# AdaLN transformer layer on one core: another order of the work in the first of eight attention turns

## The chip, the cores and the metric

The kernel runs on one core of a Trainium2 chip. The metric is the device time of one launch in microseconds (us). Three runs of the kernel before took 980.37 to 980.84 us, with a median of 980.65.

Engines: PE is TensorE (matrix products and transposes), DVE is VectorE, ACT is ScalarE, POOL is GpSimd, and SP issues most of the DMAs. Each engine works through its own list of instructions in written order; semaphores join them.

## The reference, cut to what matters

```python
# x: (2, 1024, 256) f32; 16 query heads in 4 groups, 4 key/value heads, D = 128
mod = (silu(c) @ wmod).reshape(2, 6, 1, -1)             # c: (2, 256)
sa, ca, ga, sb, cb, gb = (mod[:, i] for i in range(6))
ga = (2 * (ga >= 0) - 1) * maximum(abs(ga), 0.25)        # gb in the same way
h = layernorm(x) * (1 + ca) + sa
qkv = einsum('bsh,ph->bsp', h, weight_qkv)               # per group: 4 q, k, v
scores = einsum('bsgqd,btgd->bgqst', q, k) / sqrt(128)   # causal
attn = softmax(scores)
x = x + ga * (einsum('bgqst,btgd->bsgqd', attn, v) @ weight_proj.T)
h = layernorm(x) * (1 + cb) + sb
h = fwht(h * SU_ug) / 64
h = silu(h @ W_gate.T * s_gate) * (h @ W_up.T * s_up)
h = fwht(h * SU_dp) / 64
x = x + gb * (h @ W_down.T * s_down)
```

## The kernel before, in words

Every f32 factor of a product is split in a high part (fp32r) and a low part (the rest), and a product is three matmuls: high by high, high by low, low by high (`three`, L922 to L924). Names end in `_hi` and `_lo`.

The attention goes in eight turns, one for each batch and key/value head. A turn has twelve chunks (`C`): a chunk is 512 positions of one q head, of k or of v, made by six matmuls of 512 columns from h_hi, h_lo, w_hi and w_lo. ScalarE takes the high part from PSUM (L588 to L592) and VectorE the low part (L786, L788). Then come, for each tile of 128 queries and each of 4 heads, the scores (`S`: PE L1031 to L1037, DVE adds the mask and finds the maximum in L820, ACT makes the exp in L603, POOL divides by the sum in L493 and L496), the transposes of the probabilities (`T`: PE L1046, ACT L623, DVE L824), the products with v (`V`) and the projection (`Y`). The score tiles alternate between two PSUM areas of two banks each, so a score waits for the exp of the second one before it. v is transposed by `VT` (PE L999, ACT L581, DVE L794).

What order these take is a list of steps, `WALK`, built by `walk()` (L64 to L137). All four compute engines go through the same list, and each does its own part of a step. What stands before the loop over `WALK` in an engine's code is done first.

Turn 0 has extra work ahead. SP loads x in four quarters, the modulation weights in two parts and the first qkv weights w_raw. PE makes the first modulations (SA, CA), and the first batch's LayerNorm runs in two halves of 512 positions, each half in two slots: DVE takes statistics (`ln_front`, L714 to L722) and normalises (`ln_normalise`, L730), POOL makes rstd (L430), PE transposes (L946), ACT modulates (`ln_modulate`, L568), DVE makes h_hi (`ln_high`, L738) and POOL h_lo (`ln_low`, L437). POOL makes w_hi (`split_w`, L441) and DVE w_lo (L750). Chunk 0 needs w_lo and the first half's h_lo. The second half's transposes are the step `L0`. Three more steps belong to turn 0: `M` makes the other modulations on PE (L933, L970) and DVE copies them (L765, L766); `G` are the gates (DVE, L773 to L777, with `guard`, L704 to L707), which ga_row and so the scaling of the projection weights need; `WM` is that scaling (POOL, `scale_wp`, L476) and `WP` the split of the scaled weights (POOL, `split_wp`, L484 and L486). `gates` also waits for the five small loads, the mask among them.

After the eight turns the feed-forward part follows, which the change doesn't touch.

## Time and profile before

| | |
|---|---|
| median of three runs | 980.65 us |
| the profiled execution | 982.66 us |
| its span in the trace | 980.9 us |
| mean granted TensorE clock | 0.993 of full |
| PE busy | 941.8 us, 96% |
| DVE busy | 645.0 us, 66% |
| ACT busy | 514.3 us, 52% |
| POOL busy | 462.9 us, 47% |

The span is the time from the first to the last instruction that the profiler saw; the device time is a little longer. A row of a timeline gives start, duration, engine, line, operation, output and inputs, their shapes, and in brackets how long the engine sat idle before it and what it waited for. `PEclk` is the clock that TensorE was granted, as a share of 2.4 GHz. "ps" is a PSUM bank, and "prob" is a large buffer that in turn 0 also holds the modulation weights and the second LayerNorm slot.

### The profile page before, as it was taken

To read this page: it belongs to the slowest core of one execution; us is meant where nothing else is said; L and a number is where in the kernel's file an instruction comes from. 1 tells how busy PE (TensorE), PEld (TensorE's weight loads), DVE (VectorE), ACT (ScalarE), POOL (GpSimd) and SP (SyncE) were. 2 spreads that over 40 slices of the span, in tenths; PEclk is the share of its full clock that TensorE was granted. 3 is DMA by queue.
4 is the path that set the end of the run, shared out by engine and by line. 5 is a ranking of instruction groups with operands and counts; after the bars stand their busy time and mean duration, and the time that the engine had idled before them with its cause. 6 is when DMAs were issued, how large, how long until landed. Compare 5 with 4: busy or idle time off the path is not lost.

```text
span 980.9 us, 14522 instructions
## 1 busy us (share of the span) xinstructions
PE 941.8 (96%) x5344; PEld 818.8 (83%) x5344; DVE 645.0 (66%) x1298; ACT 514.3 (52%) x1069; POOL 462.9 (47%) x601
## 2 busy tenths in 40 slices
PE   2969999999999999999999999999999999999997
PEld 2859888888888888888888888888888887888885
DVE  5367756775677567757774787477747776864553
ACT  1346645665566456646664666366646665331221
POOL 2165634673477357725672567266716674120000
PEclk9998999999999999999999999999999999999999
DMA  8000000000000000000000000000000002000000
GB/s 303 1 1 22 1 33 1 22 2 33 1 22 1 33 1 22 1 33 1 22 4 29 2 22 21 12 1 23 1 1 1 1 20 78 1 3 20 21 21 21
DMA packets 9522, 21.14 MB, mean 22 GB/s; under 512 B 1264, under 2 KB 5488, under 8 KB 9328
## 3 DMA queue, kind: packets, MB, share of 16 engines
q1 hardware_dynamic: 8592, 19.66, 5.9%
q8 instruction: 40, 0.66, 0.3%
q10 hardware_dynamic: 864, 0.60, 0.2%
q14 instruction: 26, 0.21, 0.1%
HBM read 18.17 MB, written 2.10 MB: 21 GB/s over the span
## 4 chain that ended last, share of the span: by engine, by line
PE 87%; DVE 7%; ACT 3%; DMA 1%; issue 1%; POOL 0%; SPq 0%; DVEq 0%; ACTq 0%
PE ps L922 18%; PE ps L924 18%; PE ps L923 18%; PE ps L1046 11%; PE ps L1031 6%; PE ps L1037 6%; PE ps L1034 6%; DVE ps L820 3%; ACT prob L603 2%; DVE pt_lo L824 1%; DMA x<-in_x 1%; PE ps L946 1%; PE ps L999 1%; PE ps L1091 1%; ACT pt_hi L623 0%
## 5 line engine op out<-in xcount | busy, mean ns | idle before, releaser
L493 POOL TENSOR_TENSOR rinv<-rsum,mone 128x1 f32<-128x1 f32 x256 | 143.4, 560 | 290.6 <-ACT prob L603 290.4
L623 ACT ACTIVATE pt_hi<-ps 128x512 fp32r<-128x512 f32 x288 | 171.8, 597 | 136.2 <-PE ps L1046 135.1
L824 DVE TENSOR_TENSOR pt_lo<-ps,pt_hi 128x512 fp32r<-128x512 f32 x288 | 198.3, 689 | 64.4 <-ACT pt_hi L623 62.7
L603 ACT ACTIVATE prob<-ps,nmax 128x1024 f32<-128x1024 f32 (+7 forms) x256 | 189.8, 742 | 83.8 <-DVE nmax L820 83.0
L820 DVE CUSTOM_DVE_ANT_0 ps<-ps,mask_f 128x1024 f32<-128x1024 f32 (+7 forms) x256 | 193.9, 763 | 51.7 <-PE ps L1037 49.8
L496 POOL TENSOR_SCALAR prob<-prob,rinv 128x1024 f32<-128x1024 f32 (+7 forms) x256 | 192.5, 752 | 53.9 <-POOL rinv L493 53.9
L1046 PE MATMUL ps<-ident,prob 128*128 128x128 f32 x1152 | 172.2, 273 | 5.4 <-DVE pt_lo L824 5.4
L1046 PEld LDWEIGHTS ps<-ident,prob 128*128 128x128 f32 x1152 | 141.7, 141 | 24.8 <-DVE pt_lo L824 5.6
L922 PE MATMUL ps<-pt_hi,v_hi 128*128 128x512 f32 x288 | 134.6, 467 | 0.0
L924 PE MATMUL ps<-pt_hi,v_lo 128*128 128x512 f32 x320 | 126.5, 395 | 0.0
L1031 PE MATMUL ps<-k_hi,q_hi 128*128 128x512 f32 (+4 forms) x384 | 114.0, 351 | 6.8 <-ACT prob L603 6.8
L923 PE MATMUL ps<-pt_lo,v_hi 128*128 128x512 f32 x288 | 113.7, 395 | 0.0
L1037 PE MATMUL ps<-k_hi,q_lo 128*128 128x512 f32 (+4 forms) x384 | 111.3, 344 | 0.0
L1034 PE MATMUL ps<-k_lo,q_hi 128*128 128x512 f32 (+4 forms) x384 | 110.9, 343 | 0.0
L922 PE MATMUL ps<-h_hi,w_hi 128*128 128x512 f32 x192 | 79.1, 412 | 11.2 <-POOL h_lo L437 11.2
L1031 PEld LDWEIGHTS ps<-k_hi,q_hi 128*128 128x128 f32 x384 | 70.1, 190 | 23.4 <-ACT prob L603 10.6
L788 DVE SCALAR_TENSOR_TENSOR q_lo<-ps,q_hi 128x512 fp32r<-128x512 f32 x64 | 44.2, 691 | 62.0 <-ACT q_hi L592 62.0
L1034 PEld LDWEIGHTS ps<-k_lo,q_hi 128*128 128x128 f32 x384 | 71.3, 190 | 7.8
L592 ACT ACTIVATE q_hi<-ps 128x512 fp32r<-128x512 f32 x64 | 38.3, 599 | 74.9 <-PE ps L924 74.9
L924 PE MATMUL ps<-h_hi,w_lo 128*128 128x512 f32 x192 | 76.0, 396 | 0.0
L923 PE MATMUL ps<-h_lo,w_hi 128*128 128x512 f32 x192 | 75.9, 395 | 0.0
L1037 PEld LDWEIGHTS ps<-k_hi,q_lo 128*128 128x128 f32 x384 | 71.0, 189 | 5.3
(133 smaller groups left out, 1618.3 us busy)
## 6 DMA issues: line engine op xcount, KB each, us to landing
w_raw<-in_wqkv SPq DMA_DIRECT2D x8, 768.0 KB, 4.2
wp_raw<-in_wproj SPq DMA_DIRECT2D x8, 512.0 KB, 3.5
x<-in_x SPq DMA_DIRECT2D x4, 512.0 KB, 10.9
prob<-in_wug SPq DMA_DIRECT2D x4, 512.0 KB, 4.8
out_y<-prob SPq DMA_DIRECT2D x4, 512.0 KB, 2.9
prob<-in_wmod SPq DMA_DIRECT2D x1, 1024.0 KB, 11.6
raw_down<-in_wdn SPq DMA_DIRECT2D x1, 1024.0 KB, 12.6
prob<-in_wmod SPq DMA_DIRECT2D x1, 512.0 KB, 5.5
```

Of the source, the lines that this page charges most:

```text
L496: g_.tensor_scalar(row(i, h), row(i, h), rinv[:, at, h:h + 1], 1.0, ALU.mult, ALU.mult).then_inc(prob_done, 1)
L603: a_.activation(row(i, h).rearrange("p (a n) -> p a n", a=nb), score_banks(i, h).rearrange("p (a n) -> p a n", a=nb)[:, :, 0:w], ACT.Exp, ...
L623: a_.activation(pt_hi[:, n % 3, :], ring(t, "T", n), ACT.Copy).then_inc(pth_done, 1)
L820: v_.tensor_tensor_reduce(scores, scores, late, -1.0, 3.0e38, ALU.add, ALU.min, nmax[:, place(n), h:h + 1]).then_inc(max_done, 1)
L824: v_.tensor_tensor(pt_lo[:, n % 3, :], ring(t, "T", n), pt_hi[:, n % 3, :].bitcast(F32), ALU.subtract).then_inc(ptl_done, 1)
L922: mm(dst, w_h, r_h, start=start, stop=False)
L923: mm(dst, w_h, r_l, start=False, stop=False)
L924: return mm(dst, w_l, r_h, start=False, stop=stop)
L1031: mm(dst[:, a * CH:a * CH + wide], q_hi[:, h, q_at], k_hi[:, a * w:a * w + wide], start=True, stop=False)
L1034: mm(dst[:, a * CH:a * CH + wide], q_hi[:, h, q_at], k_lo[:, a * w:a * w + wide], start=False, stop=False)
L1037: last = mm(dst[:, a * CH:a * CH + wide], q_lo[:, h, q_at], k_hi[:, a * w:a * w + wide], start=False, stop=True)
L1046: last = tr(ring(t, "T", n)[:, q * P:(q + 1) * P], row(i, q, j * P, (j + 1) * P), ident[:, :])
```

## The change

Only turn 0 takes another order.

- Both v chunks go to the end of the turn's chunks, and chunks 0 to 7 use the four score banks, chunks 8 to 11 the two banks of `X`. Before, chunks went round six banks.
- The second half's LayerNorm: DVE takes its statistics only after it has made the first half's h_hi and h_lo; its transposes stand behind chunk 1, its h_hi and h_lo in a new step `LH0` behind chunk 2.
- The first batch's h_lo is made by DVE, no longer by POOL.
- DVE copies the first modulations before it makes w_lo, and POOL makes w_hi before the second half's rstd.
- `M` stands behind chunk 3 (before: behind chunk 7), `G` behind chunk 6, and `WM` and `WP` behind chunk 7 (before, these three stood behind the first score of tile 6).
- Each of the last four chunks is followed by a score of tile 7; the four small scores of tile 0 all stand behind `VT`.
- SP's queue: the mask, which ACT's queue had, stands behind the modulation weights; quarters 2 and 3 of x and raw_down stand behind the first projection weights.
- The wait for x's last quarters moves from the gates to step `LF`, that for the small loads on ACT behind the attention.

```diff
@@ -43,7 +43,7 @@
 QS = [[("q", h, half) for h in range(QPG)] for half in range(2)]
-CHUNKS_FIRST = [("k", 0, 0)] + QS[0] + [("v", 0, 0), ("k", 0, 1)] + QS[1] + [("v", 0, 1)]
+CHUNKS_FIRST = [("k", 0, 0)] + QS[0] + [("k", 0, 1)] + QS[1] + [("v", 0, 0), ("v", 0, 1)]
 CHUNKS_LATER = [("k", 0, 0), ("k", 0, 1)] + QS[1] + [("v", 0, 0), ("v", 0, 1)] + QS[0]
@@ -75,14 +75,15 @@
     s7 = scores(0, NT - 1)
-    out = [(0, "C", 0, 0), (0, "L0", 0, 0)] + [(0, "C", c, 0) for c in range(1, 8)] + [(0, "M", 0, 0)]
-    out += [(0, "C", c, 0) for c in (8, 9)] + [s7[0], (0, "C", 10, 0), s7[1], (0, "C", 11, 0), s7[2], s7[3]]
-    out += scores(0, 0)[:2]
+    out = [(0, "C", 0, 0), (0, "C", 1, 0), (0, "L0", 0, 0), (0, "C", 2, 0), (0, "LH0", 0, 0), (0, "C", 3, 0), (0, "M", 0, 0)]
+    out += [(0, "C", c, 0) for c in (4, 5, 6)] + [(0, "G", 0, 0), (0, "C", 7, 0), (0, "WM", 0, 0), (0, "WP", 0, 0)]
+    for h in range(QPG):
+        out += [(0, "C", 8 + h, 0), s7[h]]
     for t in range(TURNS):
...
         rest = [(t - 1, "Y", i, 0) for i in WINDOWS[-1][::-1]] if t else []
-        out += rest[:1] + [(t, "VT", 0, 0)] + s0[2 + (t > 0):] + [s6[0]] + rest[1:]
-        out += [(t, "WP", 0, 0)] if t else [(t, "G", 0, 0), (t, "WM", 0, 0), (t, "WP", 0, 0)]
+        out += rest[:1] + [(t, "VT", 0, 0)] + s0[3 if t else 0:] + [s6[0]] + rest[1:]
+        out += [(t, "WP", 0, 0)] if t else []
         behind, due = [], []
@@ -297,8 +298,8 @@
         def bank(t, c):
-            if t == 0:
-                return X[c % 6 - 4] if c % 6 >= 4 else S[c % 6 // 2][:, c % 2 * CH:(c % 2 + 1) * CH]
+            if t == 0 and c >= 8:
+                return X[c % 2]
             return S[c % 4 // 2][:, c % 2 * CH:(c % 2 + 1) * CH]
@@ -388,14 +389,16 @@
             load_wmod(1)
-            load_x(2)
-            load_x(3)
-            sp.dma_start(raw_down[:, :], wdn).then_inc(raw_s[4], 16)
+            sp.dma_start(mask_f[:, :], mask_in).then_inc(small_s, 16)
             for t in range(TURNS):
...
                              wproj[t % NKV, :, :].rearrange("p (h n) -> p h n", h=QPG)).then_inc(wpraw_s, 16)
+                if t == 0:
+                    load_x(2)
+                    load_x(3)
+                    sp.dma_start(raw_down[:, :], wdn).then_inc(raw_s[4], 16)
                 if t + 1 < TURNS:
@@ -441,18 +444,15 @@
             for r, slots in enumerate(LN_SLOTS):
-                pool.sem_inc(ln[r]["lo"], slots)
+                if r:
+                    pool.sem_inc(ln[r]["lo"], slots)
             pool.wait_ge(pool_self, 1)
...
                 ln_rstd(0, 0, 0, slot)
+            pool.wait_ge(wraw_s, 16)
+            split_w()
             for slot in range(2):
...
-
-            pool.wait_ge(wraw_s, 16)
-            split_w()
-            for g in range(NP // 2):
-                for slot in range(2):
-                    ln_low(0, 0, g, slot)
@@ -552,7 +552,6 @@
             a_.activation(sc[:, 1, :, :], sc[:, 0, :, :], ACT.Exp, scale=-1.0).then_inc(silu_e, 1)
-            act.dma_start(mask_f[:, :], mask_in).then_inc(small_s, 16)
             act.dma_start(su_u[:, :], su_ug).then_inc(small_s, 16)
@@ -571,10 +570,8 @@
             act.wait_ge(mod_ok, 1)
-            for g in range(NP // 2):
-                for slot in range(2):
-                    ln_modulate(0, 0, g, slot)
-            act.wait_ge(small_s, 5 * 16)
+            for slot in range(2):
+                ln_modulate(0, 0, 0, slot)
             def v_high(t):
@@ -609,6 +606,9 @@
                     exps()
+                if what == "L0":
+                    for slot in range(2):
+                        ln_modulate(0, 0, 1, slot)
                 if what == "VT":
@@ -627,6 +627,7 @@
+            act.wait_ge(small_s, 5 * 16)
             a_.activation(sc[:, 1, :, :], sc[:, 0, :, :], ACT.Silu)
@@ -682,6 +683,7 @@
                 dve.sem_inc(s, n)
+            dve.sem_inc(ln[0]["lo"], LN_SLOTS[0])
             dve.sem_inc(g32_s, 2)
@@ -737,27 +739,32 @@
+            def ln_low(r, b, g, slot):
+
+                n, block, _, _ = ln_step(r, b, g, slot)
+                dve.wait_ge(ln[r]["hi"], n + LN_SLOTS[r] + 1)
+                at = slice(block * P, (block + LP) * P)
+                v_.tensor_tensor(h_lo[:, :, at], h32[slot][:, :, :], h_hi[:, :, at].bitcast(F32), ALU.subtract).then_inc(ln[r]["lo"], 1)
+
...
+
+            dve.wait_ge(mod_mm, 1)
+            link(v_.tensor_copy(cols[:, 0:2, :, :], S[0][:, 0:2 * KH * B].rearrange("p (v k b) -> p v k b", v=2, k=KH)))
+            v_.tensor_scalar(cols[:, CA, :, :], cols[:, CA, :, :], 1.0, None, ALU.add).then_inc(mod_ok, 1)
+            dve.wait_ge(w_hi_s, 1)
+            v_.tensor_tensor(w_lo[:, :, :], w_raw[:, :, :], w_hi[:, :, :].bitcast(F32), ALU.subtract).then_inc(w_ready, 1)
+            for slot in range(2):
+                ln_high(0, 0, 0, slot)
+                ln_low(0, 0, 0, slot)
             dve.wait_ge(x_in_s[1], 16)
...
-
-            dve.wait_ge(w_hi_s, 1)
-            v_.tensor_tensor(w_lo[:, :, :], w_raw[:, :, :], w_hi[:, :, :].bitcast(F32), ALU.subtract).then_inc(w_ready, 1)
-
-            dve.wait_ge(mod_mm, 1)
-            link(v_.tensor_copy(cols[:, 0:2, :, :], S[0][:, 0:2 * KH * B].rearrange("p (v k b) -> p v k b", v=2, k=KH)))
-            v_.tensor_scalar(cols[:, CA, :, :], cols[:, CA, :, :], 1.0, None, ALU.add).then_inc(mod_ok, 1)
-            for slot in range(2):
-                ln_high(0, 0, 0, slot)
             for slot in range(2):
                 ln_normalise(0, 0, 1, slot)
-            for slot in range(2):
-                ln_high(0, 0, 1, slot)
@@ -776,7 +783,6 @@
                                       ws_d[:, :].unsqueeze(2).to_broadcast([P, KH, B]), ALU.mult))
-                dve.wait_ge(x_in_s[2], (B - 1) * NC_B * 16)
@@ -800,11 +806,16 @@
                     modulations()
+                if what == "LH0":
+                    for slot in range(2):
+                        ln_high(0, 0, 1, slot)
+                        ln_low(0, 0, 1, slot)
                 if what == "G":
...
                 if what == "LF":
+                    dve.wait_ge(x_in_s[2], (B - 1) * NC_B * 16)
                     dve.wait_ge(add_done, this(add_done, t, 0))
@@ -960,8 +971,6 @@
-                for c in (4, 5):
-                    pe.wait_ge(*evicted(0, c))
                 pe.wait_ge(wmod_s[1], 16)
@@ -978,12 +987,12 @@
                     pe.wait_ge(ln[1]["lo"], t + 1)
-                if t == 0 and c % 6 == 0:
-                    pe.wait_ge(ln[0]["lo"], LN_SLOTS[0] + 2 + c // 3)
-                if t == 0 and c == 10:
+                if t == 0 and c in (0, 5):
+                    pe.wait_ge(ln[0]["lo"], LN_SLOTS[0] + (4 if c else 2))
+                if t == 0 and c in (8, 9):
                     pe.wait_ge(mods_read, 1)
-                if c >= (4 if t else 6):
-                    pe.wait_ge(*evicted(t, c - (4 if t else 6)))
+                elif c >= 4:
+                    pe.wait_ge(*evicted(t, c - (2 if t == 0 and c > 9 else 4)))
                 at = {"q": h, "k": QPG, "v": QPG + 1}[what] * D
@@ -1019,8 +1028,7 @@
                     elif e <= QPG and not t:
-                        for c in (2 * e + 4, 2 * e + 5) if e <= 2 else (e + 6,):
-                            pe.wait_ge(*evicted(t, c))
+                        pe.wait_ge(*evicted(t, e + 5))
                     if e > 2:
```

The next rows are lists of instructions with their waits, in an engine's order.

DVE before chunk 0, kernel before: from the second half's statistics to its normalising; h32 and prob are the two slots' modulated values.

```order
L722 TENSOR_SCALAR vare<-mv 128x2 [waits ln0_aggr]
L750 TENSOR_TENSOR w_lo<-w_raw,w_hi 128x1536 [waits w_hi_done]
L753 COPY cols<-ps0 128x8 [waits mod_multiplied]
L754 TENSOR_SCALAR cols<-cols 128x4 [waits dve_self]
L738 CAST h_hi<-h32 128x2x256 [waits ln0_h32]
L738 CAST h_hi<-prob 128x2x256 [waits ln0_h32]
L730 TENSOR_SCALAR xhat<-x,mv,rstd 128x256 [waits ln0_rstd,ln0_tr]
```

The same place in the changed kernel.

```order
L732 TENSOR_SCALAR prob<-x,mv,rstd 128x256
L756 COPY cols<-ps0 128x8 [waits mod_multiplied]
L757 TENSOR_SCALAR cols<-cols 128x4 [waits dve_self]
L759 TENSOR_TENSOR w_lo<-w_raw,w_hi 128x1536 [waits w_hi_done]
L740 CAST h_hi<-h32 128x2x256 [waits ln0_h32]
L747 TENSOR_TENSOR h_lo<-h32,h_hi 128x2x256 [waits ln0_hi]
L740 CAST h_hi<-prob 128x2x256 [waits ln0_h32]
L747 TENSOR_TENSOR h_lo<-prob,h_hi 128x2x256 [waits ln0_hi]
L716 BN_STATS stats<-x 128x6 [waits x_loaded1]
```

The columns now stand ahead of w_lo, h_lo is new on DVE, and the second half's statistics begin behind it.

POOL from the first rstd on, kernel before.

```order
L430 TENSOR_TENSOR rstd<-vare,mhalf 128x2 [waits ln0_vare] x3
L441 TENSOR_SCALAR w_hi<-w_raw 128x1536 [waits w_raw_loaded]
L437 TENSOR_TENSOR h_lo<-h32,h_hi 128x2x256 [waits ln0_hi]
L437 TENSOR_TENSOR h_lo<-prob,h_hi 128x2x256 [waits ln0_hi]
L437 TENSOR_TENSOR h_lo<-h32,h_hi 128x2x256 [waits ln0_hi]
L437 TENSOR_TENSOR h_lo<-prob,h_hi 128x2x256 [waits ln0_hi]
L493 TENSOR_TENSOR rinv<-rsum,mone 128x1 [waits exp_done]
```

The changed kernel, the same place.

```order
L433 TENSOR_TENSOR rstd<-vare,mhalf 128x2 [waits ln0_vare]
L444 TENSOR_SCALAR w_hi<-w_raw 128x1536 [waits w_raw_loaded]
L433 TENSOR_TENSOR rstd<-vare,mhalf 128x2 [waits ln0_vare] x2
L476 TENSOR_TENSOR wp_raw<-wp_raw,ga_row 128x1024 [waits wp_raw_loaded,gate_ready]
L484 TENSOR_SCALAR wp_hi<-wp_raw 128x1024 [waits y_done,wp_scaled]
L486 TENSOR_TENSOR wp_lo<-wp_raw,wp_hi 128x1024 [waits wp_hi_done]
L493 TENSOR_TENSOR rinv<-rsum,mone 128x1 [waits exp_done]
```

w_hi stands ahead of the second two rstd, the four h_lo are gone, and the scaling and the split of the projection weights stand ahead of the first score's normalising.

DVE at the gates, kernel before: behind the maximum of tile 6's first score (896 columns).

```order
L820 ISA ps0,nmax<-ps0,mask_f 128x2x448 [waits scores_done]
L820 ISA nmax 128x1
L773 TENSOR_SCALAR cols<-cols 128x4 [waits small_loaded,modulations_read]
L704 SCALAR_TENSOR_TENSOR sum_down<-ga_row 128x512
L705 TENSOR_SCALAR sum_down<-sum_down 128x512 [waits dve_self]
L706 TENSOR_SCALAR sum_down<-ga_row 128x512 [waits dve_self]
L707 SCALAR_TENSOR_TENSOR ga_row<-sum_down 128x512 [waits dve_self]
```

DVE at the gates in the changed kernel: from q_lo of chunk 6 to that of chunk 7.

```order
L794 SCALAR_TENSOR_TENSOR q_lo<-ps1,q_hi 128x512 [waits qkv_hi]
L780 TENSOR_SCALAR cols<-cols 128x4 [waits small_loaded,modulations_read]
L706 SCALAR_TENSOR_TENSOR sum_down<-ga_row 128x512
L707 TENSOR_SCALAR sum_down<-sum_down 128x512 [waits dve_self]
L708 TENSOR_SCALAR sum_down<-ga_row 128x512 [waits dve_self]
L709 SCALAR_TENSOR_TENSOR ga_row<-sum_down 128x512 [waits dve_self]
L706 SCALAR_TENSOR_TENSOR sc<-cols 128x4
L707 TENSOR_SCALAR sc<-sc 128x4 [waits dve_self]
L708 TENSOR_SCALAR sc<-cols 128x4 [waits dve_self]
L709 SCALAR_TENSOR_TENSOR cols<-sc 128x4 [waits dve_self]
L784 TENSOR_TENSOR cols<-cols,ws_d 128x4 [waits dve_self]
L794 SCALAR_TENSOR_TENSOR q_lo<-ps1,q_hi 128x512 [waits qkv_hi,dve_self]
```

The gates now stand between two chunks' low parts, and the wide maxima stand behind them.

## Rows read from the trace of the kernel before

**Rows 1.** The page's busy times: us, share of the span, instructions.
```profile
PE 941.8 (96%) x5344; PEld 818.8 (83%) x5344; DVE 645.0 (66%) x1298; ACT 514.3 (52%) x1069; POOL 462.9 (47%) x601
```

**Rows 2.** PE's timeline, 7 to 79 us: start, us, engine, line, what.
```profile
7.31 3.54 PE L933 MATMUL ps<-sc,prob 128*128 128x2 f32 x16 [7.31 <-DMA prob<-in_wmod]
...
11.60 1.06 PE L946 MATMUL ps<-ident,prob 128*128 128x128 f32 x4
23.82 0.76 PE L922 MATMUL ps<-h_hi,w_hi 128*128 128x512 f32 x1 [11.16 <-POOL h_lo L437]
...
37.62 2.73 PE L933 MATMUL ps<-sc,prob 128*128 128x2 f32 x24
...
42.16 0.99 PE L922 MATMUL ps<-h_hi,w_hi 128*128 128x512 f32 x1
...
46.40 0.62 PE L1031 MATMUL ps<-k_hi,q_hi 128*128 128x512 f32 x2
...
47.76 0.39 PE L922 MATMUL ps<-h_hi,w_hi 128*128 128x512 f32 x1
...
73.84 1.11 PE L1046 MATMUL ps<-ident,prob 128*128 128x128 f32 x4 [5.40 <-DVE pt_lo L824]
...
78.98 0.50 PE L922 MATMUL ps<-pt_hi,v_hi 128*128 128x512 f32 x1
```

**Rows 3.** DVE's timeline before chunk 0.
```profile
12.19 0.75 DVE L714 BATCH_NORM_STATS2 stats<-x 128x6 f32<-128x256 f32 x2 [2.23 <-DMA x<-in_x]
...
17.04 1.76 DVE L750 TENSOR_TENSOR w_lo<-w_raw,w_hi 128x1536 fp32r<-128x1536 f32 x1 [2.25 <-POOL w_hi L441]
...
20.17 0.43 DVE L738 CAST h_hi<-h 128x512 fp32r<-128x512 f32 x1 [1.09 <-ACT h L568]
```

**Rows 4.** POOL's timeline: w_hi, then scaling and split of projection weights.
```profile
15.54 1.48 POOL L441 TENSOR_SCALAR w_hi<-w_raw 128x1536 fp32r<-128x1536 f32 x1
...
68.47 2.34 POOL L476 TENSOR_TENSOR wp_raw<-wp_raw,ga_row 128x1024 f32<-128x1024 f32 x1
71.00 1.05 POOL L484 TENSOR_SCALAR wp_hi<-wp_raw 128x1024 fp32r<-128x1024 f32 x1 [0.19 <-issue]
72.13 2.35 POOL L486 TENSOR_TENSOR wp_lo<-wp_raw,wp_hi 128x1024 fp32r<-128x1024 f32 x1
```

**Rows 5.** SP's timeline: the issue of w_raw.
```profile
2.27 0.47 SPq L388 DMA_DIRECT2D w_raw<-in_wqkv  x1
```

**Rows 6.** DMAs: queue, count, KB each, us from issue to landing.
```profile
w_raw<-in_wqkv SPq DMA_DIRECT2D x1, 768.0 KB, 7.9
...
mask_f<-in_mask ACTq DMA_DIRECT2D x1, 512.0 KB, 7.9
```

**Rows 7.** DVE's timeline: the first wide maximum, and the gates.
```profile
47.96 1.23 DVE L820 CUSTOM_DVE_ANT_0 ps<-ps,mask_f 128x1024 f32<-128x1024 f32 x1
...
65.20 0.17 DVE L773 TENSOR_SCALAR cols<-cols 128x4 f32<-128x4 f32 x1
...
67.52 0.16 DVE L704 SCALAR_TENSOR_TENSOR sc<-cols 128x4 f32<-128x4 f32 x1
...
68.57 2.27 DVE L706 TENSOR_SCALAR sc<-cols 128x4 f32<-128x4 f32 x1
...
71.07 0.99 DVE L777 TENSOR_TENSOR cols<-cols,ws_d 128x4 f32<-128x4 f32 x1
```

**Rows 8.** ACT's timeline: the mask's issue, the first wide exp.
```profile
2.48 0.33 ACTq L555 DMA_DIRECT2D mask_f<-in_mask  x1
...
49.81 1.11 ACT L603 ACTIVATE prob<-ps,nmax 128x1024 f32<-128x1024 f32 x1
```

**Rows 9.** Windows: stretch, length, busy time by engine, PEclk, DMA share, GB/s.
```profile
58.50:62.00 3.50, 3.27 (x17) 2.98 (x15) 1.89 (x7) 1.65 (x4) 2.88 (x6) 0.51 0.00 0
68.50:72.00 3.50, 0.00 (x0) 0.00 (x0) 3.40 (x4) 0.00 (x0) 3.31 (x3) 1.00 0.00 0
74.00:78.50 4.50, 4.50 (x15) 3.83 (x16) 2.24 (x4) 2.45 (x6) 3.56 (x5) 0.50 0.41 117
```

## The prediction

> **What bounds the kernel now.** I read the busy shares first: TensorE (PE) is busy for 941.8 of 980.9 us [rows 1], so 39 us are not matmul time, and a change of order alone can win only among them and among stretches at half clock. Then PE's timeline of the first 80 us, because the change touches only turn 0 (every other turn keeps its chunk order, banks and waits). There PE makes the modulations at 7.31, the eight LayerNorm transposes until 12.66, and then does nothing for 11.16 us, until chunk 0 at 23.82 [rows 2]. In the first 79 us it also stops for 5.40 us before the transposes at 73.84 [rows 2], and it has short stops in the scores' chain. The engines' own timelines say why. In the first gap everything hangs on VectorE (DVE), in its written order: statistics of the second half's x (its data land at 12.19), the low half of the weights at 17.04, the columns of the modulations, then h_hi at 20.17 [rows 3]. GpSimd (POOL) made w_hi only at 15.54, since the second half's rstd stands ahead of it [rows 4]; but w_raw was issued at 2.27 and landed 7.9 later, at 10.17 [rows 5, 6]. The second gap is DVE in the gates from 65.20 to 72.06 [rows 7], while scores, their maxima and pt_lo queue behind.
>
> I count up to one landmark: the start of the second P·V group of turn 0, at 78.98 [rows 2]. Behind it PE runs full in both versions, so what the landmark gains, the end gains.
>
> **First part: until chunk 0.** The mask's 0.5 MB were moving from 2.48 to 10.38 [rows 6, 8], beside x, the first modulation weights and w_raw. Now the mask goes behind them. Total bytes until 10.4 fall by about a sixth, so w_raw lands between 9.0 and 10.17 instead of at 10.17; the first modulations may start up to 0.6 earlier. DVE has normalised the first half ahead of PE's transposes and is free. PE's modulations end at 10.85 (7.31+3.54), its transposes at 12.66 [rows 2]. Now: columns copied and 1 added by about 11.3; w_hi (1.48 [rows 4]) from 9.2 to 10.7 at best, to 11.9 at worst; w_lo (1.76 [rows 3]) then ends at 13.1, at worst 13.8. ScalarE's modulation of slot 0, which follows its transposes, lies beside w_lo. Then DVE: h_hi 0.43 [rows 3] and h_lo, twice. DVE's h_lo has no row; by w_lo's 1.76 for 1536 columns it is 0.59 to 0.7 for 512 (estimate from rows 3). Twice 0.43+0.69 with three short waits on itself is 2.5. Chunk 0 starts at 15.6 (15.0 to 16.4) instead of 23.82: **8.2 us earlier**.
>
> **Second part: the chunks.** A chunk is six matmuls of 512 columns. PE starts one score of six such matmuls at 46.40 and the next chunk at 47.76 [rows 2], so 1.36 for six at full clock; at half clock twice, 2.6. Chunk 0 starts cold, as before: I take 4.3 us at half clock, nearly the 4.5 us behind the other long stop [rows 9], then full. Chunks 0 and 1 take 4.85; eight transposes at full clock 1.0 (four take 1.06 cold [rows 2], so eight 2.1, halved); chunks 2 and 3 2.7; the later modulations 4.5, as before (37.62 to 42.16 [rows 2]); and the two chunks behind them 4.24, since the two before (42.16 to 46.40 [rows 2]) ran at half clock behind the same small matmuls; chunks 6 and 7 2.7. That is 20.1, so chunk 7 ends at 35.7. The same place was 43.8 with the clock's dip moved to where it now is: the 8.2 stay.
>
> What hides the moved work: DVE ends h_lo at 15.5. The second half's fronts take 2.6 (from 12.19 [rows 3] to 14.8, one rstd of 0.7 ahead of w_hi's 15.54 [rows 4]), to 18.1; rstd and normalising end at 19.6; PE reaches these transposes at 15.6+4.85 = 20.4. Margin 0.8; what it lacks is paid one to one. The second half's h_hi and h_lo, now on DVE between q_lo of chunk 2 and of chunk 3, end near 27; chunk 5, which reads them, starts at 30.9. Cost nothing; if the cover went, up to 4 us later would still be free. ScalarE's four activations of the second half come between its evictions of chunks 1 and 2 and end by 23.3, before that of chunk 2 is due. x, quarters 2 and 3, and raw_down go behind wp_raw on SP's queue; their readers come after 80 us. Nothing.
>
> **Third part: the gates.** They now stand in DVE's order ahead of q_lo of chunk 7. q_lo of chunk 6 ends at 35.8. The row part takes 2.3 (65.20 to 67.52 [rows 7]), so gate_ready comes at 38.1, and POOL, idle since the second rstd, scales wp_raw (2.34, to 40.5), makes wp_hi (1.05, 40.7 to 41.8) and wp_lo (2.35, to 44.2) [rows 4]. The five tiny operations behind the row part are 0.16 each, but in the trace two kinds of them wait for POOL: the tensor_scalar at 68.57 lasts 2.27, until the scaling ends, and the tensor_tensor at 71.07 lasts 0.99, until wp_hi (71.00+1.05) ends [rows 4, 7]. The same pattern, started at 38.2, gives 40.5 and 41.8. So q_lo of chunk 7 ends at 42.5. PE is through chunk 8, score 0 and chunk 9 at 35.7+4.1 = 39.8, and score 1 waits for that q_lo: **a stop of 2.75 us in place of the 5.40**.
>
> The scalar_tensor_tensor at 67.52 took 0.16 in the middle of a POOL operation on SBUF [rows 7]; its two inputs are both in SBUF. The Trainium skill (SBUF — State Buffer, Who interferes with whom) says that VectorE and GpSimd lock a shared port pair for a whole instruction, also where VectorE has two SBUF inputs. The tensor_scalar and tensor_tensor rows agree, this row doesn't; by the page the sum would be that of the second rival below.
>
> **Fourth part: the scores.** From 42.55 each score's chain is: PE 1.36, maximum 1.23 and 0.1 to 0.2 around it, exp 1.11 and about 0.2 for its sum [rows 7, 8]. Before, chunks 10 and 11 alone covered these; scores 2, 3 and the four small ones stood bare. Now a chunk lies between each two scores. DVE makes maximum 0 by 44.4, exp 0 ends 45.65. Score 1 42.55 to 43.9, chunk 10 to 45.2, score 2 45.7 to 47.1 (waits 0.5 for exp 0), chunk 11 to 48.4, score 3 to 49.8, v's transposes to about 51. exp 3 is done at 52.6, so small scores 1 to 3 go 52.6 to 53.7. DVE does v_lo (until 54.4) ahead of their four maxima, so exp of small score 2 is done at 56.1, and the first score of tile 6 starts there: a stop of 2.4. Two tile-6 scores and the first transposes to 59.0; the third waits for an exp until 60.0; it and two transposes to 61.6+0.4. Behind these the P·V group, a score and a transpose lead to the landmark: 64.5 at full clock.
>
> Now the clock. It was at half (0.51 of 2.4 GHz) from 58.5 to 62.0, after the sparse small scores, and at 0.50 from 74.0 to 78.5, after the long stop; but after 3.5 us of idling (68.5 to 72.0) it was still full [rows 9]. The sparse stretch comes again (51 to 56), and I take one half-clock spell on the tile-6 scores, 1.1. For the 2.75 us stop I take 1.0, half of what a spell on score 1 and chunk 10 costs (six matmuls more at 0.2 each, twice, 2.0 to 2.4), because the rows speak both ways; ends 0 and 2.4. Landmark 64.5+2.1 = 66.6.
>
> **Sum.** 78.98−66.6 = 12.4 us. The profiled execution took 982.66, 1.8 more than its span of 980.9, and is 2.0 above the median of 980.65. 982.66−12.4 = 970.3; less 2.0, **968.3 us**.
>
> **Rivals.**
> 1. The clock stays full in both sparse places. For: 3.5 us of idling at clock 1.00 [rows 9]. Against: the spell at 58.5. 2.1 less: 966.2. Chance 12%.
> 2. POOL catches the tiny operations once more: one of them waits for wp_hi, and then the tensor_tensor for wp_lo, until 44.2 instead of 41.8. For: start gaps of 0.1 decide. Against: in the trace the small scalar_tensor_tensor passed. q_lo of chunk 7, maximum 0 and all behind are 2.4 later, and a stop of 5.2 drops the clock: 2.4, in part with 1.0 more, 970.7 to 971.7. Chance 20%.
> 3. Half clock lasts longer: PE never gets dense between 42 and 62, so two more spells like that of 74.0 to 78.5 (4.5 us at half, 2.25 lost each [rows 9]) follow. 968.3+4.5 = 972.8. Chance 12%.
> 4. Slower than before: the mask. It was the second transfer of ScalarE's queue, landed at 10.4 and was needed at 47.96 [rows 6 to 8]. It is now behind six transfers on SP's queue, and the gates wait for all five small loads at 35.8. Each us that it lands after 35.8 costs one; from 35.8+12.4 = 48.2 on the kernel is slower; landing at 52 it would give 968.3+16.2 = 984.5. Against: ahead of it lie 3.3 MB, and the trace had w_raw there at 10.17 with 1.75 MB up to it on its queue and the mask beside them; at that rate the mask lands by 20. Chance 3%.
> 5. The order doesn't carry: the score chain from 42.5 on loses again what the chunks won (PE reaches the landmark at 79). It would need 12 us more of stops, where the chain above has 6 in all. 980.6, chance 3%.
>
> **How the numbers follow.** My forecast has 50%. Its own range is 966.5 to 970.5: chunk 0 0.6 earlier or 0.8 later, the clock ±1. The range for 8 in 10 reaches over rivals 1 to 3, 965.5 to 973.0. A measurement tells about 0.2%, 2 us, from no change. Forecast and rivals 1, 2 and 3 are all faster by more, 0.94; rival 5 is the same, 0.03; rival 4 slower, 0.03.
>
> **What would show it.** PE's chunk 0 near 15.6, its idle before that about 3 us; w_hi before 12; no idle on PE at the second half's transposes near 20.4. The gates on DVE near 36, with one long tensor_scalar of about 2.2 and one tensor_tensor of about 1.0; PE's stop before the second wide score of 2.7; a stop of about 2.4 before the first score of tile 6; no stop of 5 near 62. The second P·V group at 66.6. Wrong it would be if DVE's h_lo took over 1 us, if PE waited at the second half's transposes or at chunk 5, or if later turns' idle grew.

## The result

| | before | changed |
|---|---|---|
| median | 980.75 us (four runs, 980.37 to 981.61) | 970.38 us (four runs, 970.33 to 970.46) |
| ratio | 1 | 0.9893, 95% interval 0.9876 to 0.9910 |
| profiled execution, its span | 982.66, 980.9 us | 970.33, 968.5 us |
| second P·V group of turn 0 starts | 78.98 | 66.39 |

The kernel is 10.4 us faster, where 12.4 were forecast (968.3, range 965.5 to 973.0). In the two profiled executions, though, the span is 12.4 shorter and the landmark (the last row of the table, the point up to which the prediction counts) 12.6 earlier.

The page of the changed kernel, busy us, share and count [rows 1 before]: PE's work is the same, its idle time is 27.5 us where it was 39.

```profile
PE 941.0 (97%) x5344; PEld 817.9 (84%) x5344; DVE 644.5 (67%) x1302; ACT 513.8 (53%) x1069; POOL 456.3 (47%) x597
```

PE's timeline of the changed kernel, for [rows 2]: start, us, engine, line, what, and in brackets the idle time before.

```profile
7.12 3.55 PE L944 MATMUL ps<-sc,prob 128*128 128x2 f32 x16 [7.12 <-DMA prob<-in_wmod]
...
15.25 0.76 PE L933 MATMUL ps<-h_hi,w_hi 128*128 128x512 f32 x1 [2.78 <-DVE h_lo L747]
...
20.00 0.60 PE L957 MATMUL ps<-ident,xhat 128*128 128x128 f32 x4
...
23.62 2.76 PE L944 MATMUL ps<-sc,prob 128*128 128x2 f32 x24
26.24 3.63 PE L979 MATMUL ps<-prob,scb 128*128 128x256 f32 x8
29.44 0.66 PE L933 MATMUL ps<-h_hi,w_hi 128*128 128x512 f32 x1
...
42.32 0.73 PE L1039 MATMUL ps<-k_hi,q_hi 128*128 128x512 f32 x2 [2.90 <-DVE q_lo L794]
...
56.94 1.12 PE L1039 MATMUL ps<-k_hi,q_hi 128*128 128x448 f32 x2 [1.93 <-ACT prob L600]
...
66.39 0.48 PE L933 MATMUL ps<-pt_hi,v_hi 128*128 128x512 f32 x1
```

The idle 11.16 before chunk 0 is 2.78 now, and it hangs on VectorE's h_lo. The second half's transposes at 20.00 have no wait. The stop of 5.40 is gone; one of 2.90 stands before the second wide score, on q_lo.

VectorE's timeline: the start, and the gates [rows 3 and 7 before].

```profile
9.06 1.98 DVE L732 TENSOR_SCALAR prob<-x,mv,rstd 128x256 f32<-128x256 f32 x2 [0.34 <-POOL rstd L433]
10.96 0.15 DVE L756 COPY cols<-ps 128x8 f32<-128x8 f32 x1
11.15 0.17 DVE L757 TENSOR_SCALAR cols<-cols 128x4 f32<-128x4 f32 x1
11.23 1.75 DVE L759 TENSOR_TENSOR w_lo<-w_raw,w_hi 128x1536 fp32r<-128x1536 f32 x1
12.90 0.42 DVE L740 CAST h_hi<-h 128x512 fp32r<-128x512 f32 x1
13.35 0.69 DVE L747 TENSOR_TENSOR h_lo<-h,h_hi 128x512 fp32r<-128x512 f32 x1
...
35.25 0.16 DVE L780 TENSOR_SCALAR cols<-cols 128x4 f32<-128x4 f32 x1
...
37.76 2.37 DVE L707 TENSOR_SCALAR sc<-sc 128x4 f32<-128x4 f32 x1
40.17 0.17 DVE L708 TENSOR_SCALAR sc<-cols 128x4 f32<-128x4 f32 x1
40.37 0.97 DVE L709 SCALAR_TENSOR_TENSOR cols<-sc 128x4 f32<-128x4 f32 x1
41.38 0.17 DVE L784 TENSOR_TENSOR cols<-cols,ws_d 128x4 f32<-128x4 f32 x1
41.58 1.29 DVE L794 SCALAR_TENSOR_TENSOR q_lo<-ps,q_hi 128x512 fp32r<-128x512 f32 x2
```

GpSimd in the same places [rows 4 before].

```profile
9.10 1.47 POOL L444 TENSOR_SCALAR w_hi<-w_raw 128x1536 fp32r<-128x1536 f32 x1 [0.15 <-DMA w_raw<-in_wqkv]
...
37.73 2.38 POOL L476 TENSOR_TENSOR wp_raw<-wp_raw,ga_row 128x1024 f32<-128x1024 f32 x1 [19.24 <-DVE ga_row L709]
40.29 1.04 POOL L484 TENSOR_SCALAR wp_hi<-wp_raw 128x1024 fp32r<-128x1024 f32 x1 [0.18 <-issue]
41.42 2.37 POOL L486 TENSOR_TENSOR wp_lo<-wp_raw,wp_hi 128x1024 fp32r<-128x1024 f32 x1
```

w_hi stands at 9.10 (before 15.54), right behind w_raw's landing. There it meets VectorE's normalising of the second slot: the two instructions at 9.06 take 1.98 together, until 11.04, where they took 0.74 before (at 9.22), with GpSimd idle. In the gates two of VectorE's operations on four elements a row end with one of GpSimd's: 37.76+2.37 with the scaling at 40.11, 40.37+0.97 with wp_hi at 41.33. The tensor_scalar at 40.17 and the tensor_tensor at 41.38 fall in the gaps between GpSimd's operations and take 0.17.

### The profile page after: what moved, and what is told of

Its sections match the earlier page's. It is cut to its first block, busy times and chain, and to the rows that moved or that the text cites. A ratio compares the mean times of both kernels' runs of the same rounds, so it can differ in the third digit from the quotient of the medians.

```text
span 968.5 us, 14525 instructions
## 1 busy us (share of the span) xinstructions
PE 941.0 (97%) x5344; PEld 817.9 (84%) x5344; DVE 644.5 (67%) x1302; ACT 513.8 (53%) x1069; POOL 456.3 (47%) x597
## 4 chain that ended last, share of the span: by engine, by line
PE 89%; DVE 7%; ACT 3%; issue 1%; DMA 0%; POOL 0%; DVEq 0%; SPq 0%; ACTq 0%
PE ps L933 19%; PE ps L935 18%; PE ps L934 18%; PE ps L1054 11%; PE ps L1039 7%; PE ps L1045 6%; PE ps L1042 6%; DVE ps L831 3%; ACT prob L600 2%; DVE pt_lo L835 1%; PE ps L957 1%; PE ps L1008 1%; PE ps L1099 1%; PE ps L1100 0%; DMA x<-in_x 0%
```

## The experiments

"Before" in each is the kernel before on the same chip, run beside the experiment: its median was 981.88 in experiments 3 to 5, 980.82 in 2 and 7 to 9, 980.47 in 6 and 10. Ratios are taken against that median, so medians of different experiments that lie 1 to 1.5 us apart tell little by themselves. These 25 executions fall in two groups: 15 took 980.0 to 981.1 at a mean clock of 0.996, 10 took 981.8 to 982.8 at 0.992 or 0.993. The diffs are shortened, and the comments in them are mine.

**1. The kernel before, a second execution with a profile.** No edit.

> The kernel before, once more, to see what one profiled execution of it stands for. Its profiled execution took 982.66 us against a median of 980.7 (2.0 more), the one of the changed kernel 970.33 against 970.38. Theory A (the 2.0 us belong to that one execution, by where the half-clock stretches fell): this execution takes 980.4 to 981.6, 1 to 2 less than 982.66; its landmark (second P.V group of turn 0, 78.98) comes 1 to 2 us earlier, with less or shorter half clock before it (three stretches before, about 41.5 to 45, 58.5 to 62 and 72 to 79). Theory B (profiling costs every execution of this kernel 2 us): 982.6 again, with the landmark at 79.0.

It took 980.22, its span is 978.4. PE's timeline of this execution at the landmark, and windows of it (stretch, length, busy time of PE, PEld, DVE, ACT and POOL, PEclk, DMA share, GB/s):

```profile
76.50 0.48 PE L922 MATMUL ps<-pt_hi,v_hi 128*128 128x512 f32 x1
```

```profile
41.50:45.00 3.50, 3.50 (x17) 2.94 (x16) 1.46 (x3) 0.60 (x1) 0.00 (x0) 1.00 0.00 0
58.50:62.00 3.50, 1.58 (x9) 1.30 (x8) 1.80 (x6) 1.35 (x6) 2.82 (x7) 1.00 0.00 0
69.20:75.90 6.70, 4.02 (x12) 3.55 (x13) 5.04 (x8) 3.17 (x6) 6.21 (x6) 0.50 0.28 79
```

The landmark is 2.48 us earlier than in [rows 2], the span 2.5 shorter. The stretch behind the small modulation matmuls (41.5 to 45) and the one behind the small scores ran at full clock here, where the first profile had half (0.51 from 58.5 to 62.0 [rows 9]); only that at the gates' stop is left. Counted in steps of 1 us up to 90, the clock read half for about 14 us in the first profile and about 7 here. Theory A holds, if by a little more than I gave (980.22 against 980.4 to 981.6, the landmark 2.5 earlier against 1 to 2): the 2.0 us between profile and median were half clock in that execution. It is no oddity, though: it belongs to the longer of the two groups above, 10 of 25.

**2. The changed kernel again.** No edit.

> The changed kernel once more, beside the kernel before on one chip. Theory A (half-clock stretches fall differently from execution to execution, in both kernels, and cost each up to 3 us): the single times spread over 969 to 972, the medians differ by 10 to 12. Theory B (the changed kernel is steady, its first four times lay within 0.13 us): all at 970.3 to 970.5.

Single times 967.46, 970.25, 970.54 and 970.95, median 970.40; ratio 0.9891 (0.9875 to 0.9906). The profile is of the 967.46, with a span of 965.7. Its landmark and three of its windows:

```profile
63.51 0.48 PE L933 MATMUL ps<-pt_hi,v_hi 128*128 128x512 f32 x1
```

```profile
26.20:29.60 3.40, 3.40 (x17) 2.89 (x16) 0.77 (x2) 0.42 (x1) 0.00 (x0) 1.00 0.00 0
43.20:46.70 3.50, 3.39 (x16) 2.81 (x16) 1.78 (x4) 2.02 (x4) 3.01 (x4) 1.00 0.32 128
52.40:59.20 6.80, 5.62 (x17) 5.00 (x18) 2.57 (x9) 2.58 (x10) 4.12 (x9) 0.50 0.00 0
```

The same stretches in the profile of the 970.33:

```profile
26.20:29.60 3.40, 3.40 (x11) 2.77 (x10) 0.36 (x1) 0.00 (x0) 0.00 (x0) 0.50 0.00 0
43.30:46.70 3.40, 3.40 (x9) 2.65 (x9) 2.50 (x5) 1.21 (x2) 1.60 (x3) 0.50 0.49 148
56.90:60.30 3.40, 3.36 (x9) 3.02 (x10) 0.71 (x1) 0.34 (x2) 2.66 (x7) 0.50 0.00 0
```

The 967.46 is an execution without half clock in the modulations and behind the 2.90 stop (which is there, 2.91); in exchange its half clock on tile 6 lasts longer. By the starts of PE's steps the modulations took 4.2 in place of 5.8, score 1 and chunk 10 3.1 in place of 4.45, and from the first tile-6 score to the landmark 9.9 in place of 9.45; the cold stretch from chunk 0 on was 0.6 shorter. B falls. Of A the core holds, that the stretches fall differently, but not its range: seven of the eight times lie between 970.25 and 970.95, and the eighth lies 1.5 below the 969 that I gave.

**3. The changed start alone.** On the kernel before: POOL's and DVE's code ahead of the loop and SP's queue as in the changed kernel, steps as before.

```diff
-                ln_rstd(0, 0, 1, slot)
-            pool.wait_ge(wraw_s, 16)
-            split_w()
-            ... ln_low(0, 0, g, slot)          # POOL, all four
+            pool.wait_ge(wraw_s, 16)
+            split_w()
+                ln_rstd(0, 0, 1, slot)
...
+            # DVE: columns, w_lo, ln_high and ln_low of the first half, then ln_front(0, 0, 1, slot)
```

> The kernel before with the changed start alone: w_hi ahead of the second rstd, modulation columns ahead of w_lo, h_lo on VectorE, statistics of the second half behind the first half's h_lo, and the new DMA order; its chunks, gates and scores stand as before, the second half's transposes behind chunk 0. Chunk 0 should start at 15.25, as in the changed kernel, 8.6 earlier than 23.82. The second half's transposes then wait for VectorE at about 18.3 and 19.4 (chunk 0 ends at 17.95), 1.0 lost. Theory A (the parts add; the gain carries through): 980.7-7.6 = 973.1, and the 5.4 us stop at the gates stays. Rival (the start isn't what sets the end; the score chain and gates are tied to other work, so a start 8 us earlier is given back there): 976 to 980.

974.33 (972.69 to 974.67); ratio 0.9923 (0.9909 to 0.9936), so 7.6 us with an interval of 6.3 to 8.9. By groups it is 7.8 and 7.9: four times of 974.2 to 974.7 at clock 0.992 or 0.993 against 982.3 before, one of 972.69 at 0.996 against 980.6. PE's timeline of it:

```profile
15.10 0.77 PE L928 MATMUL ps<-h_hi,w_hi 128*128 128x512 f32 x1 [2.77 <-DVE h_lo L744]
...
18.27 1.09 PE L952 MATMUL ps<-ident,xhat 128*128 128x128 f32 x4 [0.27 <-DVE xhat L729]
...
65.92 1.12 PE L1052 MATMUL ps<-ident,prob 128*128 128x128 f32 x4 [5.38 <-DVE pt_lo L830]
```

Chunk 0 is where it was expected, and the gates' stop is unchanged at 5.38. Theory A: most of a start 8.7 us earlier (15.10 against 23.82) passes through to the end. The rival's 976 to 980 didn't come. The median is 1.2 above my 973.1, inside the interval.

**4. The gates back behind the first score of tile 6**, in the changed kernel.

```diff
-    out += [... (4, 5, 6)] + [(0, "G", 0, 0), (0, "C", 7, 0), (0, "WM", 0, 0), (0, "WP", 0, 0)]
+    out += [... (4, 5, 6)] + [(0, "C", 7, 0)]
-        out += [(t, "WP", 0, 0)] if t else []
+        out += [(t, "WP", 0, 0)] if t else [(t, "G", 0, 0), (t, "WM", 0, 0), (t, "WP", 0, 0)]
+                dve.wait_ge(small_s, 5 * 16)        # in the copy of the modulations
```

> The changed kernel with the gates, the scaling and the split of the projection weights back behind the first score of tile 6 (VectorE waits for the small loads in the copy of the modulations instead). The 2.90 us stop of TensorE before the second wide score goes, and its half clock; score chain 1.4+1.4 each from 39.2 on, so the fourth wide score ends near 45.5 instead of 50.9. A stop of about 5 us before the third transposes comes back, with half clock behind it (2.4). Theory A: 4 to 5 won in the chunks, 7 to 7.5 lost behind, 970.4+2.5 = 973. Rival (where the gates stand makes no difference, VectorE needs the same time for them): 970.4.

971.81, single times 967.04, 970.78, 972.84 and 972.98; ratio 0.9904 (0.9888 to 0.9919). The median is 1.4 above the changed kernel's and 2.5 below experiment 3; the interval overlaps those of both. The place of the gates alone is no clear gain here, and neither theory A (973) nor the rival (970.4) is decided. The profile is of the 967.04, and the stop before the third transposes is 2.03 there, not 5. VectorE and GpSimd in it:

```profile
54.43 0.16 DVE L781 TENSOR_SCALAR cols<-cols 128x4 f32<-128x4 f32 x1
...
57.20 0.17 DVE L708 TENSOR_SCALAR sc<-cols 128x4 f32<-128x4 f32 x1
57.40 0.16 DVE L709 SCALAR_TENSOR_TENSOR cols<-sc 128x4 f32<-128x4 f32 x1
57.60 0.92 DVE L785 TENSOR_TENSOR cols<-cols,ws_d 128x4 f32<-128x4 f32 x1
```

```profile
57.50 1.01 POOL L496 TENSOR_SCALAR prob<-prob,rinv 128x896 f32<-128x896 f32 x1 [0.21 <-POOL rinv L493]
58.47 2.35 POOL L476 TENSOR_TENSOR wp_raw<-wp_raw,ga_row 128x1024 f32<-128x1024 f32 x1
```

GpSimd was late, so the tiny operations were through before the scaling began, all but the last, which waits out a normalising (57.50+1.01): 4.1 us for the gates, not 6.9. My expectation had taken the 5 us stop as fixed; in this execution it was 2.03. No profile shows the three longer ones. Their mean clock was lower too (0.994, 0.992 and 0.992 against 0.996), so how much of the 3.7 to 5.9 us that they are longer is the meeting with GpSimd and how much the clock is open.

**5. The tiny operations first**, in the changed kernel.

```diff
-                guard(ga_row[:, :, :], guard_a, guard_b).then_inc(gate_ok, 1)
-
                 link(guard(cols[:, GB, :, :], sc[:, 2, :, :], sc[:, 3, :, :]))
                 link(v_.tensor_tensor(cols[:, GB, :, :], cols[:, GB, :, :],
                                       ws_d[:, :].unsqueeze(2).to_broadcast([P, KH, B]), ALU.mult))
+                guard(ga_row[:, :, :], guard_a, guard_b).then_inc(gate_ok, 1)
```

> The changed kernel with the five tiny operations on the gate of the second half (gb) ahead of the gate row, not behind it; nothing else. They then run while GpSimd is idle: 1.0 us instead of 4.0 (37.57 to 41.55), and gate_ready comes 1.0 later, at 38.6. q_lo of chunk 7 ends at 39.3 instead of 42.2, TensorE's stop of 2.90 before the second wide score nearly goes, and with it the half clock from 43.4 to 46.5 (1.6). Theory A: 970.4-4.4 = 966.0. Rival (the stop only moves on to the exp of the second wide score and the small scores, which are bound by maximum and exp): 968 to 970.

966.11 (964.52 to 967.21); ratio 0.9843 (0.9830 to 0.9856). That is 4.3 below the changed kernel (by ratios 4.9), with intervals that lie apart. The landmark, and VectorE's timeline:

```profile
60.49 0.48 PE L932 MATMUL ps<-pt_hi,v_hi 128*128 128x512 f32 x1
```


```profile
33.26 0.16 DVE L780 TENSOR_SCALAR cols<-cols 128x4 f32<-128x4 f32 x1
33.33 0.15 DVE L706 SCALAR_TENSOR_TENSOR sc<-cols 128x4 f32<-128x4 f32 x1
...
35.97 0.69 DVE L709 SCALAR_TENSOR_TENSOR ga_row<-sum_down 128x512 f32<-128x512 f32 x1
36.58 1.28 DVE L793 SCALAR_TENSOR_TENSOR q_lo<-ps,q_hi 128x512 fp32r<-128x512 f32 x2
```

The gates last from 33.26 to 36.6, 3.3 us in place of 6.3, and q_lo follows. TensorE's stop of 2.90 before the second wide score is gone; of the stops of over 1 us behind chunk 0 those of 1.40 and 1.93 before tile 6 are left. Theory A: VectorE's waiting for GpSimd was the stop. The profiles to compare are this one and that of experiment 2, since both have one half-clock stretch of about 7 us, on tile 6 (PEclk 0.52 from 49.5 to 56.3 here): the landmark comes at 60.49 instead of 63.51 and the span is 962.7 instead of 965.7, so 3.0 us are the stop. What the medians show above that fits the half clock behind it, but no pair of profiles shows it apart.

**6. The same in the old place** (experiments 4 and 5 together).

> The gates in their old place behind the first score of tile 6, as in the run gates_back (967.0 to 973.0 there, 4.1 us for the gates in its profile, against 6.9 in the kernel before), with the five tiny operations ahead of the gate row. Theory A (the spread there is whether the tiny operations meet GpSimd's scaling; with them first they can't): the gates take 3.4 to 4.4 us in every execution, the spread shrinks to 3 us or less, median 966 to 967.5. Theory B (the spread is half clock alone): again 967 to 973 with a median near 971.

968.07, single times 966.91 to 968.88; ratio 0.9872 (0.9856 to 0.9888). The spread is 2.0 where it was 5.9, and the median is 0.6 above the range that I gave for theory A and 3 below that for B. That favours A, on four executions each, without showing it: the two profiled executions (967.04 in experiment 4, 967.36 here) are alike, with 4.1 us for the gates, stops of 2.03 and 2.12, and landmarks 48.0 behind chunk 0, so the gain lies in executions that no profile shows. Nor is the meeting with GpSimd gone: the last operation on the gate row takes 1.39 for 0.69 here, across a normalising. Set beside experiment 5 the place among the chunks is worth 2.0 by medians and 2.8 by ratios, with intervals that just touch.

**7. The small scores ahead of v's transposes as well.** Experiment 5, and in `walk()`:

```diff
-        out += rest[:1] + [(t, "VT", 0, 0)] + s0[3 if t else 0:] + [s6[0]] + rest[1:]
+        out += rest[:1] + ([(t, "VT", 0, 0)] + s0[3:] if t else s0 + [(t, "VT", 0, 0)]) + [s6[0]] + rest[1:]
```

> The kernel with the tiny gate operations first (966.1), and in addition all four small scores of tile 0 ahead of v's transposes in turn 0. VectorE then takes their maxima before v_lo, and TensorE has the transposes of v (1.0) to do where it stood for 1.93 us before the first score of tile 6; the wait of 1.40 before the second small score stays, and one of 0.5 for the first. Theory A (the stop before tile 6 is VectorE's order, v_lo ahead of the maxima): 1.1 less, 965.0. Rival (the exps set it, and the clock's half stretch behind it stays anyway): 966.1, no change.

964.97, single times 965.18, 965.34, 964.97, 961.99 and 962.11; ratio 0.9819 (0.9802 to 0.9837). The 1.93 stop before tile 6 is gone from the trace; the half clock there is not, as the rival has it (v's transposes take 1.91 at half clock, 1.03 in the changed kernel). Against experiment 5 the 1.1 us are as expected, but the intervals overlap, so theory A is not decided by the time. The two times near 962 had a mean clock of 0.998 against 0.995; neither was profiled. It is the fastest version of all, 5.4 below the changed kernel on the same chip.

**8. h_lo on GpSimd again.**

```diff
-                ln_low(0, 0, 0, slot)        # DVE; the same in step LH0
+                ln_low(0, 0, g, slot)        # POOL: first half behind split_w(), second behind ln_rstd
```

> The changed kernel with all four h_lo of the first batch on GpSimd again, the rest as changed (w_hi first, columns first, statistics of the second half late). GpSimd takes 1.3 for one (20.68, 22.31 before) where VectorE takes 0.69, and VectorE's second h_hi waits while it runs. Theory A: chunk 0 starts at 16.6 instead of 15.25, all else shifts: 970.4+1.3 = 971.7. Rival (GpSimd's lie beside VectorE's work, so they cost nothing or gain because VectorE is freed for the statistics): 970.0 to 970.4.

971.65 (968.87 to 971.92); ratio 0.9894 (0.9879 to 0.9909). VectorE's timeline of it, in which the second h_hi waits for GpSimd's h_lo (13.33 to 14.59):

```profile
13.65 1.22 DVE L742 CAST h_hi<-prob 128x512 fp32r<-128x512 f32 x1 [0.41 <-ACT prob L570]
```

Chunk 0 starts 9.30 behind the first modulation matmul (16.36, 7.06) instead of 8.13. The median fits theory A; the time alone would not decide it, the place of chunk 0 does.

**9. The second half's statistics early.**

```diff
+            dve.wait_ge(x_in_s[1], 16)
+                ln_front(0, 0, 1, slot)
             dve.wait_ge(mod_mm, 1)
```

> The changed kernel with the second half's statistics back at their old place on VectorE, ahead of the modulation columns and of w_lo. They last 2.6 from 11.0 on; columns to 14.0, w_lo 15.7, and four h parts 2.1 more: chunk 0 at 17.9, 2.6 later than 15.25. Theory A (VectorE's order is what set chunk 0, and of the 8.6 won there 2.6 come from this one move): 970.4+2.6 = 973.0. Rival (the start is bound by the arrival of w_raw and w_hi, statistics lie in that wait): 970.4.

972.99 (972.57 to 973.31); ratio 0.9914 (0.9901 to 0.9928). PE's timeline of it:

```profile
18.37 0.76 PE L933 MATMUL ps<-h_hi,w_hi 128*128 128x512 f32 x1 [5.48 <-DVE h_lo L747]
```

It is 10.84 behind the first modulation matmul (7.53) instead of 8.13. Theory A: 2.7 of the 8.6 us that chunk 0 won are this move, and the median is 2.6 above the changed kernel's on the same chip (970.40).

**10. The mask on ScalarE's queue.**

```diff
-            sp.dma_start(mask_f[:, :], mask_in).then_inc(small_s, 16)
+            act.dma_start(mask_f[:, :], mask_in).then_inc(small_s, 16)
```

> The changed kernel with the mask on ScalarE's queue again, second there as before, so that its 0.5 MB travel beside w_raw. w_raw lands at 10.2 instead of 9.07; w_hi ends at 11.7 instead of 10.6, so w_lo starts at 11.7 instead of 11.23. Theory A (only what w_hi passes w_lo's other bound counts): chunk 0 0.5 later, 15.7, 970.4+0.5 = 970.9. Rival (w_lo is bound by the modulation columns alone, which wait for TensorE): 970.4.

970.56 (970.26 to 970.75); ratio 0.9897 (0.9880 to 0.9913). w_hi starts at 9.82 and w_lo at 11.32; chunk 0 is 8.50 behind the first modulation matmul where it was 8.13. So 0.4 in the trace, 0.2 in the medians: no difference that can be told. The mask's place earns next to nothing. One reason is in the trace: with the later w_hi VectorE's normalising at 8.81 takes 0.74 again, not 1.98, so what the earlier w_hi wins it loses in part there.

## Why the prediction was right, point by point

- **Chunk 0 at 15.6.** Measured 15.25. h_lo took the 0.69 of the estimate, w_hi started at 9.10 against 9.2 "at best". I overlooked that the early w_hi holds up VectorE's normalising until 11.04; the columns, forecast by 11.3, were ready at 11.32 all the same. Of the 8.4 us that chunk 0 won against the first modulation matmul, experiments 8 to 10 give 1.2 to h_lo on VectorE, 2.7 to the late statistics and 0.4 to the mask. About 4 are left for w_hi ahead of the second rstd and the columns ahead of w_lo, which no run tried alone.
- **The chunks, 20.1 us to 35.7.** Measured 19.9, to 35.18. The margin at the second half's transposes held: no wait at 20.00. The dip of the clock came inside the modulations (5.8 for 4.5), and the chunks behind them ran full (3.0 for 4.24): the terms were off by 1.3 and 1.2 in opposite directions, so the good sum is in part luck. (The terms as listed add up to 20.0, not 20.1.)
- **The gates.** Forecast: scaling to 40.5, wp_hi to 41.8, a stop of 2.75. Measured 40.11, 41.33 and 2.90. The pattern was not the one that I named. The tensor_scalar behind the long one slipped through, and the scalar_tensor_tensor took 0.97, until wp_hi ended: with its two SBUF inputs it does wait. The Trainium skill (SBUF — State Buffer, Who interferes with whom) says that a VectorE instruction with two SBUF inputs contends with a GpSimd instruction that reads SBUF; this trace agrees, 0.97 against 0.16. I had misread the 0.16 at 67.52 in [rows 7] as lying in the middle of a GpSimd operation. It starts 0.03 behind that operation, and the one behind it does wait:

```profile
67.49 1.02 POOL L496 TENSOR_SCALAR prob<-prob,rinv 128x896 f32<-128x896 f32 x1 [0.21 <-POOL rinv L493]
```

```profile
67.72 0.82 DVE L705 TENSOR_SCALAR sc<-sc 128x4 f32<-128x4 f32 x1
```

The last operation fell in the gap of 0.09 ahead of wp_lo, so rival 2's 2.4 us didn't come. That it fell there was a matter of 0.1 us, and by the time alone (970.38 measured, 970.7 in rival 2) it could not be told; the trace decides it.
- **The scores.** First score of tile 6 at 56.1 plus 1.0 for the clock; measured 56.94. Its stop 1.93 against 2.4.
- **The clock.** One spell of 1.1 on tile 6 came. For the 2.90 stop I took 1.0 of at most 2.4; score 1 and chunk 10 took 4.45 for 2.7, so 1.7.
- **The landmark.** 66.6 forecast, 66.39 measured. That close an agreement is luck: the second profile of the same kernel has it at 63.51, with the same work in the same order, because other stretches ran at half clock. The stops and gates came as forecast in both profiles (2.90 and 2.91, 1.93 and 1.93), and these are what the prediction had right.
- **The step that missed:** "less 2.0, 968.3 us". I took the 2.0 between the profiled execution of before and its median as a fixed part of both kernels. It was half clock of that execution (experiment 1), and part of the 12.4 that the landmark wins. The profiled execution of the changed kernel, which the landmark of 66.6 describes, had half-clock stretches as well and lay at its own median (970.33 against 970.38). Taken from the median of before, the gain is 12.4 less 2.0, and the sum 970.3; 970.38 was measured.
- **The rivals.** Rival 1 (full clock in the sparse places) came in part in single executions, as the 967.46. Rival 3 didn't; the median is nowhere near 972.8. Rival 4: the mask landed at 4.01+6.7 = 10.7, long before the gates. Rival 5: experiments 3 and 9 show that the shifts pass through.

How the 10.4 divide, each against the kernel before on its own chip, with an uncertainty of 1 us or more: the start 7.6 (experiment 3), the new order of chunks, scores and modulations 2.5 (3 to 4), the gates' place 0.3 (4 to the changed kernel; 1.4 by the plain medians). Only the first is clear of the noise. The second step holds several moves at once, and no run parts them. Not settled is how often each half-clock stretch comes; twelve profiles don't give that.

## What to carry to other kernels

A difference between one profiled execution and the median isn't a constant to subtract: look which stretches ran at half clock in it, and take a second execution if a sum rests on it. In front of the first large product each operation on the engine that everything waits for counts fully, so put there only what that product reads. And small VectorE operations on SBUF belong ahead of the instruction that starts GpSimd's long ones: here that alone gave 4.3 us by medians, 3.0 between two profiles with the same half-clock stretch.

## What the runs showed of the hardware that I had not expected

- Half-clock stretches differ between executions of one program: 982.66 and 980.22 for the kernel before, 970.33 and 967.46 for the changed one, with the landmark 2.5 and 2.9 earlier in the shorter ones.
- The small modulation matmuls, which have no gap before or behind them, ran in part at half clock in nine of the twelve profiles and at full clock in three, with the same instructions (the eight of 128x256 take 1.97 in those and 2.5 to 3.7 in the others).
- A VectorE scalar_tensor_tensor with both inputs in SBUF waits for GpSimd (0.97 for 0.16), and so does a tensor_scalar from SBUF to SBUF with one (2.37 for 0.17, 1.98 for 0.74).
- Where GpSimd is late, the same gates take 4.1 instead of 6.9 us. In that order one execution was 5.9 shorter than another (experiment 4); how much of that is this meeting and how much the clock is not shown.
